# Rotary embedding of the query: three VectorE products from PSUM in place of one product, a ScalarE partition swap and a GpSimd product

## The reference

```python
h = take(weight, x)                        # (8, 512, 256)
h = h + attn(layernorm(h), wq, wk, wv, wo)
h = h + ffn(layernorm(h), Wr, W1, b1, W2, b2)

# in attn
q = rope(einsum('btm,mhd->bthd', x, w_aq)); k = rope(... w_ak); v = ...
# rope: even, odd = halves of the head's 128 dims
#   concatenate([even * cos - odd * sin, even * sin + odd * cos])
s = einsum('bihd,bjhd->bhij', q, k) / 128 ; causal mask ; p = softmax(s)
r = einsum('bhij,bjhd->bihd', p, v) @ wo
```

## Time and profile before

| | |
|---|---|
| median of 3 runs | 1214.71 us (1210.06, 1214.71, 1214.72) |
| the profiled execution's own time | 1208.61 us |
| its span | 1206.8 us |
| busy in the span | PE 1115.3, PEld 982.2, DVE 807.7, ACT 707.7, POOL 816.8 us |
| mean granted TensorE clock | 0.973 |

### The profile page before, as it was taken

One profiled execution on the slowest core, in us unless ns is written; L12 is line 12 of the kernel. 1 busy time (PEld: TensorE's weight loads), 2 busy tenths in 40 slices (PEclk: granted clock), 3 DMA queues, 4 the chain that ended last, 5 costly groups with the idle time before them and its releaser, 6 DMA issues. The chain is left out here.

```text
span 1206.8 us, 19986 instructions
## 1 busy us (share of the span) xinstructions
PE 1115.3 (92%) x7000; PEld 982.2 (81%) x7000; DVE 807.7 (67%) x1913; ACT 707.7 (59%) x1492; POOL 816.8 (68%) x894
## 2 busy tenths in 40 slices
PE   3899999999999999999999988129999999999997
PEld 2788888888888888888888874028999999999996
DVE  4787877877787887877777756775555554554433
ACT  3667677677676676676776754005455554555642
POOL 3897897897897898887987851025484574654525
PEclk9999999999999999999999999559999999999999
DMA  5000100100100100200100003312452443524213
GB/s 196 1 19 1 45 27 1 45 27 1 45 27 1 51 21 1 70 2 30 41 1 36 19 1 111 109 30 62 106 132 32 119 103 48 132 37 105 31 23 35
DMA packets 42211, 58.10 MB, mean 48 GB/s; under 512 B 8896, under 2 KB 34944, under 8 KB 41984
## 3 DMA queue, kind: packets, MB, share of 16 engines
q0 software_dynamic: 13824, 21.24, 9.8%
q1 hardware_dynamic: 28288, 35.58, 8.8%
HBM read 35.71 MB, written 16.91 MB: 44 GB/s over the span
## 5 line engine op out<-in xcount | busy, mean ns | idle before, releaser
L271 ACT ACTIVATE prob<-prob,row_min 128x512 f32<-128x512 f32 (+3 forms) x256 | 141.7, 555 | 107.2 <-DVE row_min L435 107.2
L1170 DVE TENSOR_TENSOR hT_lo<-hid,hT_hi 128x512 fp32r<-128x512 f32 x124 | 86.7, 700 | 167.6 <-ACT hT_hi L1326 167.6
L1323 ACT ACTIVATE hid<-up,b_e 128x512 f32<-128x512 f32 x128 | 88.1, 688 | 152.4 <-PE up L1432 139.6
L908 POOL DMA_INDIRECT x<-routed_rows,tokens x64 | 85.0, 1328 | 100.4 <-DVE tokens L1164 83.0
L199 POOL TENSOR_SCALAR prob<-prob,row_inv 128x512 f32<-128x512 f32 (+3 forms) x256 | 133.6, 535 | 8.1 <-DVE row_inv L442 5.5
L207 POOL TENSOR_TENSOR q_sin<-q_sin,rope_t 128x512 f32<-128x512 f32 x64 | 82.6, 1290 | 77.2 <-ACT q_sin L295 77.1
L374 DVE TENSOR_TENSOR pT_lo<-bank,pT_hi 128x384 fp32r<-128x384 f32 (+1 forms) x192 | 109.2, 595 | 20.4 <-ACT pT_hi L253 20.3
L919 POOL TENSOR_SCALAR y<-y,gate 128x256 f32<-128x256 f32 x60 | 32.2, 549 | 127.9 <-issue 127.2
L435 DVE CUSTOM_DVE_ANT_0 prob<-bank,mask_row 128x512 f32<-128x512 f32 (+3 forms) x256 | 114.9, 486 | 2.2 <-PE bank L569 0.2
L928 POOL DMA_INDIRECT out<-y,tokens x60 | 96.0, 1600 | 16.2 <-issue 13.9
L623 PE MATMUL bank<-ident,prob 128*128 128x128 f32 x640 | 101.6, 273 | 1.5 <-POOL prob L199 0.9
(11 more groups left out here) (260 smaller groups left out, 3814.9 us busy)
## 6 DMA issues: line engine op xcount, KB each, us to landing
raw<-in_w SPq DMA_DIRECT2D x16, 1024.0 KB, 8.8
emb_res<-emb SPq DMA_DIRECT2D x8, 512.0 KB, 3.7
out<-h SPq DMA_DIRECT2D x8, 512.0 KB, 2.9
routed_rows<-x SPq DMA_DIRECT2D x8, 512.0 KB, 3.0
x<-in_wq SPq DMA_DIRECT2D x1, 1024.0 KB, 5.2
x<-in_wk SPq DMA_DIRECT2D x1, 1024.0 KB, 5.0
x<-in_wv SPq DMA_DIRECT2D x1, 1024.0 KB, 7.2
x<-in_wo SPq DMA_DIRECT2D x1, 1024.0 KB, 9.9
```

The lines of the kernel that those rows point to most:

```text
L271: nc.scalar.activation(pr, pr, ACT.Exp, bias=row_min[:, h % 2, k:k + 1], scale=-1.0, accum_out=row_sum[:, h % 2, k:k + 1]).then_inc(s["exp ...
L1170: nc.vector.tensor_tensor(out, in_, hi.bitcast(F32), ALU.subtract)\
L1323: nc.scalar.activation(hid[:, t % 2, :], up_ps[t % 2][:], ACT.Gelu, bias=bias)
```

## The change

`rope_q` and `turn_k` become one function `rotate(b, h, x)` on VectorE, which does for q what `turn_k` did for k: the product with the cosines and two products of 64 partitions with the sines, read from the other half of the PSUM bank. ScalarE's `swap` is gone, and so is GpSimd's product L207. The semaphores `q_mul`, `q_swap` and `q_sin` are replaced by `q_rope`; TensorE waits for it, where it waited for `q_swap`, before it writes bank 0 again (`xt`, `values`).

```diff
             def add(b, h, x):
                 n = b * H + h
-                if x == "q":
-                    cos, sin = q_cos, q_sin
-                    after(pool, "q_swap", n + 1)
-                    nc.gpsimd.tensor_tensor(sin[:], sin[:], rope_t[:, 1, :], ALU.mult)\
-                        .then_inc(s["q_sin"], 1)
-                    after(pool, "q_sin", n + 1)
-                else:
-                    cos, sin = k_cos, k_sin
-                    after(pool, "k_rope", n + 1)
+                cos, sin = (q_cos, q_sin) if x == "q" else (k_cos, k_sin)
+                after(pool, f"{x}_rope", n + 1)
                 nc.gpsimd.tensor_tensor(cos[:], cos[:], sin[:], ALU.add).then_inc(s[f"{x}_add"], 1)
...
-            def swap(b, h):
-                n = b * H + h
-                after(act, "q_mul", n + 1)
-                after(act, "q_add", n)
-                nc.scalar.activation(q_sin[0:64, :], proj_ps[0][64:128, :], ACT.Copy)
-                nc.scalar.activation(q_sin[64:128, :], proj_ps[0][0:64, :], ACT.Copy)\
-                    .then_inc(s["q_swap"], 1)
...
-                    if live:
-                        swap(b, h)
...
-            def rope_q(b, h):
-                n = b * H + h
-                after(dve, "q_proj", n + 1)
-                after(dve, "q_lo", n)
-                nc.vector.tensor_tensor(q_cos[:], proj_ps[0][:], rope_t[:, 0, :], ALU.mult)\
-                    .then_inc(s["q_mul"], 1)
-
-            def turn_k(b, h):
-                n = b * H + h
-                ps = proj_ps[1]
-                after(dve, "k_proj", n + 1)
-                after(dve, "k_lo", n)
-                nc.vector.tensor_tensor(k_cos[:], ps[:], rope_t[:, 0, :], ALU.mult)
-                nc.vector.tensor_tensor(k_sin[0:64, :], ps[64:128, :], rope_t[0:64, 1, :], ALU.mult)
-                nc.vector.tensor_tensor(k_sin[64:128, :], ps[0:64, :], rope_t[64:128, 1, :], ALU.mult)\
-                    .then_inc(s["k_rope"], 1)
+            def rotate(b, h, x):
+                n = b * H + h
+                ps, cos, sin = (proj_ps[0], q_cos, q_sin) if x == "q" else (proj_ps[1], k_cos, k_sin)
+                after(dve, f"{x}_proj", n + 1)
+                after(dve, f"{x}_lo", n)
+                nc.vector.tensor_tensor(cos[:], ps[:], rope_t[:, 0, :], ALU.mult)
+                nc.vector.tensor_tensor(sin[0:64, :], ps[64:128, :], rope_t[0:64, 1, :], ALU.mult)
+                nc.vector.tensor_tensor(sin[64:128, :], ps[0:64, :], rope_t[64:128, 1, :], ALU.mult)\
+                    .then_inc(s[f"{x}_rope"], 1)
...
                     if live:
-                        rope_q(b, h)
+                        rotate(b, h, "q")
                     if ok(h - 2):
                         after(dve, "exp_done", TB * (n - 2) + 4)
                         inverse(b, h - 2, 3, 4)
                     if live:
-                        turn_k(b, h)
+                        rotate(b, h, "k")
...
-                    after(pe, "k_rope" if kt else "q_swap", b * H)
+                    after(pe, "k_rope" if kt else "q_rope", b * H)
...
-                after(pe, "k_rope" if i else "q_swap", n + 1)
+                after(pe, "k_rope" if i else "q_rope", n + 1)
```

More of the change, by code:

```diff
@@ L88, in build_attention @@
             ids_in emb_in res_in stats_done aggr_done var_eps rstd_done xn_ready xt_tr xt_hi xt_lo
-            q_proj k_proj v_proj q_mul q_swap q_sin k_rope q_add k_add q_hi k_hi q_lo k_lo v_hi v_lo
+            q_proj k_proj v_proj q_rope k_rope q_add k_add q_hi k_hi q_lo k_lo v_hi v_lo
             s_done s_min exp_done inv_done norm_done t_done t_hi t_lo o_done o_hi o_lo
```

## The result

| | before | after |
|---|---|---|
| median | 1214.72 us (4 runs) | 1239.74 us (1238.56 to 1240.85, 4 runs) |
| profiled execution, its span | 1208.61, 1206.8 us | 1239.39, 1237.6 us |
| ratio | | 1.0211, 95% interval 1.0192 to 1.0229 |

The change costs 25 us on the medians and 31 between the two profiled executions. The lower figure is the one with an interval; one run of before, three times as long as the others, is left out of the ratio. In the later comparisons, on other chips, the kernel before gave 1208.4 to 1211.7 us in 45 of 46 runs, so that against those the loss would be 30. The traces give a third figure, for attention alone: the last q projection starts at 723.70 and not at 697.59, 26.1 us later.

What follows compares the result with a forecast made beforehand. TensorE was taken to set attention's pace. New stalls of 21.7 us (six middle batches), 1.95 (batch 0) and 3.3 (batch 7), together 27.0, less 7.3 of old waits, gave net +19.7 and a forecast of 1233 us, range 1222 to 1244.

Steps and rivals of the forecast that it cites:

- Direction and mechanism: Attention: VectorE's added q products bring oT_lo past its 0.44 us slack, so TensorE's output product stalls; net +19.7 us.
- sign of being wrong: Attention's plain slot (no side work or late start): still at 10.55 us, or over 11, would refute the forecast.
- other signs: Attention: q_cos to k_cos 2.08 us, oT_lo waits over 20, longest in slot 3, VectorE about 91, PE about 97 of 100.
- The term of the plain slot: Attention slots without side work: oT_lo 0.68 us later against a slack of 0.44, so each gets 0.24 us longer.
- The terms of slots 4 and 6: Middle batch, slots with a shift ahead of oT_lo: stalls of 0.65 us in slot 4 and 0.57 in slot 6.
- Slot 3: Middle batch, slot after evacuate: q_cos starts 2.46 us in, stall 1.02 us, hidden before by the 0.64 wait for k.
- Slot 7: Middle batch, slot without values: output due at 8.03 us, the chain gives 8.69, a stall of 0.66 us.
- What goes: Attention: ScalarE's waits for k_cos (12.7 us) and late norm blocks vanish; gain inside TensorE's 7.3 us of weight-load waits.
- Batch 0: First attention batch: slots 3 to 7 stall 1.95 us in all; its first slots, running on the weights' arrival, 0.
- Lateness that builds up: Rival, chance 0.10: attention slots pass delay on; 0.2 us more in 56 slots would add 11, about 1245 us.
- Occupancy: Rival, chance 0.07: VectorE's products fall into its gaps in attention; gains and losses within 4 us, 1214 us.
- GpSimd's queue as the hidden bound: Rival, chance 0.04: attention's plain slots lose nothing and the shorter sum chain gives back 7.3 us, 1207 us.

Runs made afterwards that it cites:

- e1: The changed kernel with the first row minimum moved ahead of k's three products; 1216.67 us median, ratio 1.0060 to the kernel before.
- e3: The changed kernel without the first of q's two sine products of 64 partitions; 1203.89 us in one run.
- e4: The changed kernel with GpSimd again doing a 128x512 product for every q, result not used; 1244.15 us in one run.
- e9: The kernel before with the moves of e1 and e5 (first minimum earlier, side work later); 1211.19 us median, ratio 1.0002.
- e10: e5's kernel with GpSimd again doing a 128x512 product for every q, result not used; 1213.97 us, ratio 1.0028 to the kernel before.
- e7: The changed kernel with a third, useless product of 64 partitions for q behind q_cos; 1272.13 us in one run.
- e5: e1's kernel with VectorE's side work (statistics, shift) moved from ahead of oT_lo to behind pT_lo; 1203.26 us median, ratio 0.9941 to the kernel before.
- e2: The kernel before with the first row minimum moved ahead of k's products, as in e1; 1213.62 us median, ratio 1.0030.
- e6: The kernel before with only VectorE's side work moved behind pT_lo, as in e5; 1210.20 us median, ratio 0.9997.
- e8: The changed kernel with q's two 64-partition products reading the same partitions they write; 1236.52 us in one run.

## Why the prediction was right, point by point

- **Direction and mechanism.** Right. The output product waits for `oT_lo` in every slot but slot 0, the chain from the minimum is as long as before, and `q_cos` starts at 1.68 in plain slots; e1 and e3 show that chain and slack make the loss. 19.7 us were forecast, 25 measured. The time lies in the range of 1222 to 1244. But the forecast's own sign of being wrong, a plain slot over 11, came true: it is 11.03 where 10.8 was named. Of the other signs the waits (26.4 us for `oT_lo`, the longest in slot 3) and TensorE's 97 of 100 us came as said; `q_cos` to `k_cos` (2.21 for 2.08) and VectorE's 91 (86.3) didn't. The range held all the same, by its width and because the errors below in part cancel: over slots with nothing late a middle batch is 4.3 us longer for 3.62 forecast, with 0.9 too little in slots 1, 2, 3, 5 and 7 and 0.2 too much in 4 and 6.
- **The term of the plain slot was half of what it is**: 0.24 forecast, 0.48 measured, in two parts. `q_cos` to `k_cos` was taken as 2.08 and is 2.21: the two products take 1.41 as said, but from the second to `k_cos`, with the reciprocal between, it is 0.80 and not the 0.67 read behind a `q_cos`. So the stall is 8.81 - 8.45 = 0.36. And a stalled matmul costs more than its wait: `wo_hi` to `wo_lo` is 407.70 - 407.47 = 0.23 behind a wait and was 0.11 in the unstalled slot of the kernel before (393.11 and the row below), 0.12 more in each. The rows before the change held this: the product of the earlier trace rows is 0.39 long, the one of the earlier trace rows 0.28.

```profile
393.22 0.28 PE L569 MATMUL bank<-wo_lo,oT_hi 128*128 128x256 f32 x1
```

- **The terms of slots 4 and 6 were too high**: 0.65 and 0.57 forecast as stalls. Their output products start at 8.87 and 8.81, 0.42 and 0.36 late. The step that failed is "the `shift` takes 413.20 - 412.28 = 0.92": the length of a row that held a wait for GpSimd, which the change itself took away. Slot 6 also starts at 1.68 and not 1.94, as its aggregate fits before the last `pT_lo`.
- **Slot 3**: X 2.46 forecast, 2.29 measured; stall 1.02 against 0.96 and the 0.12. **Slot 7**: 0.66 against 0.78. The due time of 8.03 was read from a product that is 0.39 long, so had itself waited for `oT_lo`: the 0.12 is already in it.
- **What goes.** Right in kind: the waits on GpSimd's blocks and ScalarE's for `k_cos` are gone, and e4, e9 and e10 show that GpSimd's queue held them: ScalarE's wait for `k_cos` is back with 4.3 us in e4 and 8.1 in e10. Slot 5 is shorter than before (11.03 against 11.18) for all its new stall.
- **The sum.** A middle batch is 3.0 us longer; 2.4 had been forecast (3.62 less 1.2 of old stalls). Batch 0 is 4.7 longer, where 1.95 had been: its slots 1 and 2, taken as 0, are 0.7 and 0.5 longer, and slot 3 is 1.07 longer and not 0.24, as `q_cos` starts 2.31 into it and not 1.68. Together attention loses 26.1 us. The profiled pair is another 4.7 us apart, all of it behind attention, and most of that isn't the change's: of the experts' matmul `up<-e_xT0hi,w_0hi` the first and last starts are 337.7 us apart in the profiled after, 334.0 in the one before and 333.9 to 334.0 in all ten experiments, seven of which have q's sine products on VectorE.
- **Rivals.** Lateness that builds up: refuted by the table and e7 (slots 2 and 5 to 7 within 0.02 of each other). Occupancy: refuted by e1 and e5. The Trainium skill, "Perfetto Trace Analysis", section "Identifying the Most-Contended Engine", takes an engine's occupancy as a fair measure of how near it is to its limit. This case disagrees for VectorE: the kernel with 91 of 100 us is faster than those with 86 and 79. GpSimd's queue as the hidden bound was right about a gain of some 7 us being there (e3, e5), and wrong that the change would show it: the chain had to be shortened first.

## What to carry to other kernels

An added instruction on a partly idle engine is priced by the slack of the chain it is put in: find the consumer that waits last, measure how early its input is, subtract. Past the slack everything is paid in every turn, below it nothing: in e3 VectorE still has a product more than in the kernel before, and plain slots stay at 10.55; in e7 one more than in the changed kernel costs its 0.60 in each. Before such a change is dropped, look at the order on the engine: what releases another engine goes first, and side work goes behind the result that TensorE asks for, not ahead of it; here that turned 2.1% slower into 0.6% faster. In the kernel before, where this chain was on time, the same moves gained nothing (e2, e6, e9).

## What the runs showed of the hardware

- A VectorE product of 4 columns with both inputs in SBUF took 0.16 us when a GpSimd row was just ending. Begun inside a GpSimd product or sum with both inputs in SBUF, it took as long as was left of that: 0.90 and 0.99 in batch 4 before, 1.06 in e4, 0.52 and 0.82 in e3, 0.68 and 0.99 in e1, always ending within 0.03 us of it. The length of a short row can be another engine's.
- The first matmul of the output product took 0.22 to 0.23 us to the next start in every slot of batch 4 after the change where `oT_lo` came late, and 0.12 in slot 0, where it didn't.
- Products of 64 x 512 from PSUM take as long as those of 128 x 512 (0.68 to 0.69). But from the start of one row of this length to the start of the next it is either 0.60 to 0.61 or 0.68 to 0.73 us. The lower figure stands where neither the first partition read from PSUM nor the first one written changes: `q_cos` to the reciprocal in the kernel before, `extra` to `q_sin` in e7, `q_cos` to `q_sin` in e8. The higher one stands where either changes from 0 to 64 or back: `q_cos` to `q_sin` in the changed kernel, one half to the other, the second half to the reciprocal. So e8 took away one change of three, and its last read from partition 64 may be why `k_cos` comes 0.19 behind the reciprocal and not 0.08. This is a pattern of the rows; only e8 varied it, and it gained nothing.
